# Graph network on one NeuronCore: layer 1's edge coefficients made beside the first aggregation, edge counts in two PSUM banks

## The reference

```python
hb = jnp.einsum('nd,bdo->bno', h, basis)          # 4 bases (layer 0), 8 bases (layer 1)
coef = comp[etypes]                               # 8 relations (layer 0), 32 (layer 1)
m = sum over b of coef[:, b, None] * hb[b][src]
agg = segment_sum(m * norm[:, None], dst)
out = agg + bias + h @ loop_w                     # no loop_w in layer 1
```

## Time and profile before

| | us |
|---|---|
| median of 3 executions | 3120.01 |
| lowest and highest | 3112.52, 3124.88 |
| the profiled execution, its own time | 3121.2 |
| its span, first to last instruction | 3119.6 |
| L0a, first to last step | 48 to 299 |
| L0b, first to last step | 487 to 748, with 8 of 10 turns |
| L1, first to last step | 878 to 1170, with 8 of 10 turns |

### The profile page before, as it was taken

How to read it: one execution, slowest core, us unless ns; L and a number is a source line. 1 busy time by engine, 2 the same in 40 slices (tenths; PEclk the granted TensorE clock), 3 DMA queues, 4 the chain that set the end, 5 groups by cost and what they waited for, 6 DMA issues and landing times.

```text
span 3119.6 us, 43370 instructions
## 1 busy us (share of the span) xinstructions
PE 2947.4 (94%) x14533; PEld 2174.3 (70%) x14533; DVE 1774.2 (57%) x4790; ACT 1200.3 (38%) x2182; POOL 1123.3 (36%) x930
## 2 busy tenths in 40 slices
PE   6988998999979889999999999999999999999999
PEld 3334874446833457774468998799987998789987
DVE  7554323435333352444376776677766776767677
ACT  1222332112323323342254554255543554435554
POOL 3665335664456534430231113510134102431022
PEclk8999999999989999999999999999999999999999
DMA  3665526664256533322112001400113001130012
GB/s 93 173 181 145 186 71 180 172 178 116 81 155 181 160 89 102 92 90 83 55 62 73 8 31 51 131 15 8 65 44 104 15 8 65 44 105 14 8 65 81
DMA packets 129388, 279.13 MB, mean 89 GB/s; under 512 B 22617, under 2 KB 45465, under 8 KB 128145
## 3 DMA queue, kind: packets, MB, share of 16 engines
q0 software_dynamic: 40320, 132.15, 14.9%
q1 hardware_dynamic: 87408, 141.55, 14.4%
q10 hardware_dynamic: 1440, 2.62, 0.2%
HBM read 227.65 MB, written 27.46 MB: 82 GB/s over the span
## 4 chain that ended last, share of the span: by engine, by line
PE 80%; DVE 9%; issue 4%; DMA 2%; ACT 2%; POOL 1%; another core or an unknown queue 0%; SPq 0%; DVEq 0%; POOLq 0%; ACTq 0%
PE banks L159 16%; PE banks L160 16%; PE banks L161 16%; PE banks L891 15%; PE banks L2449 5%; PE banks L2113 3%; PE banks L1762 2%; PE banks L854 2%; DVE y_tile L2065 1%; DVE y_tile L2067 1%; DVE columns L2048 1%; PE banks L1020 1%; DMA yT_lo<-yT_new_lo 1%; DVE x_L L2280 1%; DVE yT_new_lo L2072 1%
## 5 line engine op out<-in xcount | busy, mean ns | idle before, releaser
L891 PE MATMUL banks<-gathered,selector 128*128 x1328 | 645.2, 612 | 49.2 <-DVE selector L941 21.1
L891 PEld LDWEIGHTS banks<-gathered,selector 128*128 128x128 f32 x1328 | 236.9, 194 | 337.2 <-issue 296.9
L918 ACT COPY G<-banks 128x512 f32<-128x512 f32 x160 | 93.6, 585 | 599.7 <-PE banks L891 448.9
L2537 ACT CAST probT<-banks 128x512 fp32r<-128x512 f32 (+2 forms) x480 | 212.1, 516 | 261.7 <-PE banks L2449 260.8
L1459 POOL TENSOR_TENSOR weight_parts<-weight_ring,weight_parts 128x512 fp32r<-128x512 f32 x130 | 187.4, 1442 | 297.5 <-ACT weight_parts L1392 297.5
L2619 DVE CUSTOM_DVE_ANT_0 prob<-banks,count_by_src 128x512 f32<-128x512 f32 (+1 forms) x480 | 258.3, 588 | 57.5 <-PE banks L161 57.5
L2545 DVE TENSOR_TENSOR probT<-banks,probT 128x512 fp32r<-128x512 f32 (+2 forms) x480 | 254.1, 585 | 52.1 <-ACT probT L2537 51.5
L159 PE MATMUL banks<-weight_parts,lhs_parts 128*128 128x512 f32 x680 | 268.2, 394 | 15.1 <-DVE lhs_parts L1403 6.3
L160 PE MATMUL banks<-weight_parts,lhs_parts 128*128 128x512 f32 x680 | 266.0, 391 | 0.0
L161 PE MATMUL banks<-weight_parts,lhs_parts 128*128 128x512 f32 x680 | 265.8, 391 | 0.0
L1418 DVE TENSOR_TENSOR lhs_parts<-G,lhs_parts 128x640 fp32r<-128x640 f32 x122 | 101.4, 832 | 274.3 <-ACT lhs_parts L1390 274.1
(11 more groups left out here) (300 smaller groups left out, 6831.8 us busy)
## 6 DMA issues: line engine op xcount, KB each, us to landing
weight_ring<-in_L_gnn_basis SPq DMA_DIRECT2D x64, 256.0 KB, 2.7
weight_ring<-in_L_gnn_bases SPq DMA_DIRECT2D x64, 256.0 KB, 2.7
x_L<-x_rows SPq DMA_DIRECT2D x50, 256.0 KB, 4.3
x_rows<-x_L SPq DMA_DIRECT2D x50, 256.0 KB, 5.3
yT_hi<-yT_new_hi SPq DMA_DIRECT2D x4, 2560.0 KB, 11.4
yT_lo<-yT_new_lo SPq DMA_DIRECT2D x4, 2560.0 KB
count_rows<-count SPq DMA_DIRECT2D x10, 640.0 KB, 4.3
count_by_dst<-count_rows SPq DMA_DIRECT2D x10, 640.0 KB, 4.3
```

What stands on the lines that cost most here:

```text
L891: pe.matmul(sums[s % BATCH], sel[:, s % SELECTORS, :], rows_of[s % BATCH], start=False, stop=False, skip_group_check=True).then_inc(*multi ...
L2537: ins = act.copy(hi, of)
```

## The change

Layer 1's coefficients are made beside L0a in place of L0b. For that they need two PSUM banks during L0a, so the edge counts use banks 4 and 5 in turn, and the coefficients bank 6 (`spread`) and bank 7 (`pick`). ACT clears the four sum banks, then the two count banks, and lays the pickers behind that. In the loop, ACT copies and clears the counts ahead of the sums. DVE waits for the clearing of the count bank ahead of the two one-hots of a step. PE works out the count bank of each step from the bank of the sums.

```diff
-    C.of_layer1 = Coefficients(C, PATH1, 32, [(C.coef["L1"], "L1_gnn_w_comp")], (4,), (5, 6), *shared)
+    C.of_layer1 = Coefficients(C, PATH1, 32, [(C.coef["L1"], "L1_gnn_w_comp")], (6,), (7,), *shared)
...
+    def count_bank(w):
+        return SUM_BANKS + (w + 1) % COUNT_BANKS
...
-        counts = [psum[:, ds(b + SUM_BANKS, 1), 0:LOW].rearrange("p t d -> p (t d)") for b in banks] if counting else []
+        counts = [psum[:, ds(within(b & COUNT_BANKS - 1, COUNT_BANKS - 1) + SUM_BANKS, 1), 0:LOW].rearrange("p t d -> p (t d)")
+                  for b in banks] if counting else []
...
+        for w in range(SUM_BANKS):
+            act.copy(psum[:, sum_bank(w), :], C.zero[:].to_broadcast([P, D])).then_inc(*cleared.inc())
+        if counting:
+            for w in range(COUNT_BANKS):
+                act.copy(psum[:, count_bank(w), 0:LOW], C.zero[:].to_broadcast([P, LOW])).then_inc(*emptied.inc())
+            M.at = counting.end
         for work in beside:
             work.lay(act.copy, laid)
...
             act.wait_ge(multiplied.semaphore.sem, over[w % BATCH])
+            if counting:
+                act.copy(counting.count[:, w, :], psum[:, count_bank(w), 0:LOW]).then_inc(*counted.inc())
             act.copy(G[:, w, :], psum[:, b, :]).then_inc(*summed.inc())
+            if counting and w + COUNT_BANKS < windows:
+                act.wait_ge(*counted(w + 1))
+                act.copy(psum[:, count_bank(w), 0:LOW], C.zero[:].to_broadcast([P, LOW])).then_inc(*emptied.inc())
             if w + SUM_BANKS < windows:
                 act.wait_ge(*summed(w + 1))
+                act.copy(psum[:, b, :], C.zero[:].to_broadcast([P, D])).then_inc(*cleared.inc())
...
         if counting:
+            dve.wait_ge(emptied.semaphore.sem, window)
...
-    turned = aggregate(C, "L0a", PATH0, 4, A["x"], G, C.tables_made, counting)
+    turned = aggregate(C, "L0a", PATH0, 4, A["x"], G, C.tables_made, counting, beside=(C.of_layer1,))
...
-    turned = aggregate(C, "L0b", PATH0, 4, hidden_rows, G, ready, beside=(C.of_layer1, own))
+    turned = aggregate(C, "L0b", PATH0, 4, hidden_rows, G, ready, beside=(own,))
```

More of the change, by code:

```diff
@@ L763 @@
 SELECTORS, AHEAD = 3 * BATCH, 2 * BATCH
-SUM_BANKS = 4
+SUM_BANKS, COUNT_BANKS = 4, 2
 def aggregate(C, name, path, nb, rows, G, ready, counting=None, beside=()):
@@ L783, in aggregate @@
     tiles_landed, multiplied = C.event(f"tiles_landed_{name}"), C.event(f"multiplied_{name}")
-    cleared = C.event(f"banks_cleared_{name}")
+    cleared, emptied = C.event(f"banks_cleared_{name}"), C.event("count_banks_cleared")
     place_free, selected, laid = C.event("gathered_free"), C.event("selected"), C.event("G_zero_act")
@@ L917, in on_act @@
             act.wait_ge(multiplied.semaphore.sem, over[w % BATCH])
+            if counting:
+                act.copy(counting.count[:, w, :], psum[:, count_bank(w), 0:LOW]).then_inc(*counted.inc())
             act.copy(G[:, w, :], psum[:, b, :]).then_inc(*summed.inc())
-            if counting:
-                act.copy(counting.count[:, w, :], psum[:, SUM_BANKS + b, 0:LOW]).then_inc(*counted.inc())
+            if counting and w + COUNT_BANKS < windows:
+                act.wait_ge(*counted(w + 1))
+                act.copy(psum[:, count_bank(w), 0:LOW], C.zero[:].to_broadcast([P, LOW])).then_inc(*emptied.inc())
             if w + SUM_BANKS < windows:
                 act.wait_ge(*summed(w + 1))
[L923 to L927, removed]
+                act.copy(psum[:, b, :], C.zero[:].to_broadcast([P, D])).then_inc(*cleared.inc())
         for n in range(NT * KC):
@@ L965, in on_dve @@
                     take(n, dve)
-    assert multiplied.base == tiles_landed.base == cleared.base == 0
+    assert multiplied.base == tiles_landed.base == cleared.base == 0 and (not counting or emptied.base == 0)
     on_pool()
@@ L1508, in __init__ @@
         self.count = M.new("count", [P, PATH0.windows, LOW])
+        self.end = M.at
         self.numbered = C.event("low_numbered")
```

## The result

The changed kernel takes 3131.57 us in the median of 16 runs (3119.44 to 3139.61), the kernel before 3120.22 in runs beside it (3107.4 to 3128.18). The ratio is 1.0036, with a 95% interval of 1.0023 to 1.0048: slower by about 11 us, where the forecast was 3119 and no change. The time lies inside the whole range (3102 to 3144), 0.6 us over the forecast's own (3110 to 3131), and the change is under the half per cent that I took as the bound; but the interval excludes no change, so the loss is real. The profiled execution took 3135.7 us, 14.5 more than that of before.

The account below looks back on a forecast made before the run. PE bounds L0b's first 148 steps; in L0a late signals delay gathers and PE runs dry. L0a 18.2 + 3.3 + 17 - 29.4 = +9.1, L0b -10: net -1 on 3121.2, 3119 as median; range 3102 to 3144, own 3110 to 3131.

Parts of the forecast that it names:

- the part on the count banks: L0a: two count banks stall PE by lateness beyond 3.5 us, +17 us (0 to 30); queued compares cost nothing further.
- I let the stalls use the room as well.: L0a: PE's 29.4 us of room was set against the bank stalls as well as the 18.2 us of added work.
- The excess of 17: L0a: signal lateness beyond the limits at window ends, 12 us in the 148 steps plus 5 in the 60 behind.
- B: Rival, chance 0.25: count banks starve DVE and stalls add to the room; L0a +28, L0b -4, 3144 us.
- L0b, -10 taken: L0b without the coefficients: 18.2 us of PE work removed, gathers limit the gain; -10 taken between -18.2 and -4.
- The start, +3.3: L0a's start: bank clearings delay PE's first step to 49.9, then 1.4 us of waiting for pickers; +3.3, bounds 0 and 5.
- Register work, nothing: L0a: four more register operations per four PE steps to find the count bank, taken as nothing, up to 3 us.
- theory 2: From the experiments: PE's added work in L0a, instruction by instruction, is the price; slower by 0.3% on either chip.
- A: Rival, chance 0.25: L0a's late bursts shrink, the moved work hides there, L0b gives nearly all back; 3105 or 3102 us.
- C: Rival sharing the forecast's 0.50: L0b bound by gathers at once, L0a hides everything; -4 + 3, no change.
- The rule on bubbles: POOL, DVE and ACT gaps released by PE: too few PSUM buffers, so halving count banks makes all 17 us loss on top.
- The clock: PE after stalls over 3 us: one slow step, about 0.9 us more each, left out of the sum.

Follow-up runs that it names:

- e6: The changed kernel, unaltered, on a chip with prompt signals: 1.0015 of the kernel before.
- e16: The changed kernel, unaltered, run again on a chip with late signals: 1.0049 of the kernel before.
- e17: The changed kernel with each compare four steps earlier in DVE's list, on a chip with late signals: 1.0019 of the kernel before.
- e18: The changed kernel with counts not copied and cleared per window, so one-hots never wait for them (output wrong), late chip: 1.0006 of the kernel before.
- e9: The kernel before with seven extra ACT tiles at every third window end of L0a, late chip: 0.9998 of its own undelayed time.
- e12: The changed kernel with compare earlier, count-bank wait behind the one-hots and first banks cleared first, on a late chip: 1.0017 of the kernel before.
- e10: The changed kernel with seven extra ACT tiles at every third window end of L0a, late chip: 1.0079 of the undelayed kernel before.
- e11: The changed kernel with each compare four steps earlier and seven extra ACT tiles at every third L0a window end, late chip: 1.0071 of the undelayed kernel before.
- e7: The changed kernel with each compare four steps earlier in DVE's list, on a prompt chip: 1.0001 of the kernel before.
- e5: The kernel before, unaltered, traced on a chip with prompt signals: 3042.96 us in its one execution.
- e1: The changed kernel with layer 1's coefficients back beside L0b, only the count banks changed, on a prompt chip: 1.0012 of the kernel before.
- all three: The changed kernel with compare earlier, count-bank wait behind the one-hots and first banks cleared first: 0.9992 of the kernel before on a prompt chip, 1.0017 on a late one.

## Why the prediction was wrong

Forecast was -1 us in the sum; the profiled execution took 14.5 more. L0a cost 18.1 where +9.1 was forecast, L0b gave 5.3 where 10 was.

**The step that failed** is in the part on the count banks: "PE's spread k waits for compare k - 1, which stands 3 steps ahead: no further price while DVE leads by a window". That lead is just what is gone when the one-hot waits: one selector was left at 120.88, and 1, 2 and 1 at the other three places. Even with prompt signals DVE can lead by no more than the rest of the next window (the row of e6). Measured: 14.4 us of such waits in the kernel after, 13.6 in e16, worth 6.3 us in the stretch and 8 to 9 in the whole (e17).

**"I let the stalls use the room as well."** The sum set 18.2 of work and 17 of stalls against 29.4 of room. Without the stalls (e18) the stretch takes 184.6 us, so of 18.2 some 10 were hidden, across two chips. With them (194.3 and 191.8) another 7 to 10 came, and PE's gaps in the stretch were back at the 17.6 and 17.8 us that compare with 17.0 before: the stalls took the room from the moved work. The excess of 17 did not come in its own terms: by the same sum over the window ends it is 6.3 in the kernel after and 1.4 in e16. What took its place is the compare's wait, which needs no signal later than 3.5 us. For L0a the sum gave +9.1; the trace has +18.1 (2.6 of start, 18.1 in the 148 steps, -2.6 in the others). My 182 to 186 for the stretch is what the kernel without the wait takes; with the wait the stretch is at B's 195, and PE is busy for 0.90 of it and not for over 0.95.

**L0b, -10 taken, bounds -18.2 and -4.** The first chip gave 6.4 in the stretch and 5.3 in all, at 1.47 us a gather (175 us over POOL's 119 in the row of the kernel after), which is L1's pace and the lower bound's. On the chip of e9 to e12 it was less: beside e9's 181.4, e12 took 177.1, e10 177.5 and e11 179.0. Prompt chips gave 17.2, the other bound. The reason for the lower bound was right and the value between them too hopeful. It leaned on late signals of 3 us at most in L0b. In the 148 steps of before that nearly holds (3.4 at a window's end, but 6.4 behind them); in the kernel after 5 window ends of the 148 steps are later than 3.5, up to 5.8.

**The start, +3.3:** 1.9 to the first matmul, as worked out (49.9 for 48.07), and 0.98 of waiting for the pickers, for 1.4 forecast. The other 0.65 of the 2.6 is the preparation. **Register work, nothing:** no run shows otherwise; theory 2 fell on prompt chips, where the unchanged instruction list without the wait gains.

**The rivals.** B had the sign and the kind, a late ACT that starves DVE, and was too large: +28 for L0a, measured +18.1. Its condition, signals later than 3.5 us at more than ten window ends, didn't come: there are 4 in L0a in the kernel after and 1 in e16, for 9 before. Four or five spreads behind a blocked list were enough for half of the loss. A's condition came in part, for in the 148 steps the kernel after has 2 such window ends for 6; its hidden work didn't. On prompt chips, without any late signals, the work still costs 15.3 us in L0a (e7 against e5), because there PE has little idle time to give: 152.4 us for the 146.5 that it needs. C was right for L0b.

**The rule on bubbles.** I discounted the rule, because in the kernel before no bank ran out. The kernel after has the waits for a bank (76.6 us of DVE's, 19 times) and loses by them (e18 against e16), and the same 4.51 us of lateness, 13 times, costs the kernel before nothing and the kernel after about 0.3 to 0.4%. The Trainium skill ("Perfetto Trace Analysis", section "Optimization Strategy") says that a gap which repeats on the engine that should be saturated can mean too few PSUM buffers; for the kernel after these runs agree. As I read both, the banks that nobody waited for had been the cover.

**The clock.** The stretch's granted clock fell to 0.92 in the kernel after, from 0.97, but e16 has the same waits and nearly the same time at 0.96. So the slow steps behind a stall are a part of the loss and not its cause. I had put them at 0.9 us a stall, one slow step as in the earlier trace rows, and left them out. One step's excess is that size (1.91 us for 1.02), but two or three steps are slow behind each of the stalls at 75.99, 120.88, 169.08 and 206.56: 7.3 us in all in the kernel after, 5.3 in e16, 1.6 before. So the sum lacked some 4 to 6 us. The Trainium skill ("TensorE: Matmul & The Clock Gate", Part 1) has the slow clock as the default, which activity lifts; the trace agrees in kind.

**Left open.** Why the signals come late on some chips; what two banks alone cost on a late chip, since e1 ran on a prompt one only; how much of its loss with made lateness is the banks' and how much the coefficients'; and whether the few us left over in e18 are the coefficients' work or noise. No version beat the kernel before by more than its interval with the counts intact; 0.9992 (0.9983 to 1.0001) for all three on a prompt chip is the nearest, and it lost 0.17% on a late one.

## What to carry to other kernels

Before you take away spare buffers, ask what their longest wait has been covering: the one engine whose release comes late decides, not its busy share. Where an in-order engine gets a new wait, follow everything queued behind it to the engines that need it, and put what another engine waits for ahead of the new wait. And idle time of the bounding engine is room only for work that is ready in just those moments; work set at fixed places of its list mostly adds.

## What the runs showed of the hardware

The same kernel takes 3118 to 3128 us in three sets of runs and 3040 to 3042 in three others, on other chips, 2.5 to 2.9% apart, at nearly the same mean clock (0.986 and 0.989). The difference lies in the aggregations alone: from L1's last step to the end it is 1949.8 and 1949.0 us. It also lies only where PE is not full. L0b's 148 steps with the coefficients take 181.1 us on a late and 181.3 on a prompt chip, PE being busy for all of them; L0a's take 176.2 and 152.4; L0b's without the coefficients 174.7 to 179.0 and about 164.

In the traces of a prompt chip ACT gets the end of a window within 0.04 us, each time. On the first chip it gets it later than 3.5 us at 9 of L0a's 40 window ends, at none in L0b's first 148 steps and at 17 of the 58 window ends in L1's first 180 steps. With the coefficients gone from L0b there are 5 in its 148 steps (3 in each of e12, e16, e17 and e18). So the change did one thing more: it took from L0b the PE work that had kept it immune, and exposed it to some 11 to 15 us of late signals, while L0a stayed exposed. That is why a move that gains 17 us in L0b on a prompt chip gains 2 to 6 on a late one.
